# Weights of expert tiles taken by pairs from two shelves, in an attention and mixture-of-experts kernel

## What is computed

```python
x = x + attention(layernorm(x), ctx, ctx, w_proj, b_proj)     # x: 8 x 512 x 256, 16 heads of 16
z = layernorm(x)
gate_logits = z @ Wg.T                                        # 8 experts
gating = softmax over the two largest of them, 0 elsewhere
h = silu(z @ W1[e].T) * (z @ W2[e].T)                         # 682 hidden columns, per expert e
x = x + sum over e of gating[e] * (h @ W3[e].T)
```

## Time and profile before

| | us |
|---|---|
| median of three runs | 885.32 (885.25 to 887.26) |
| the profiled execution, its own time | 882.82 |
| its span, first to last instruction | 881.0 |

### The profile page before, as it was taken

The page is one execution under the profiler, slowest core; times in us unless marked ns, Lnnn a source line. Parts: engine busy times, 40 slices in busy tenths (PEclk is TensorE's granted clock), DMA queues, the critical chain, the costliest instruction groups (busy, mean ns, idle before and its releaser), DMA issues.

```text
span 881.0 us, 20060 instructions
## 1 busy us (share of the span) xinstructions
PE 786.4 (89%) x6472; PEld 481.1 (55%) x6472; DVE 602.0 (68%) x1224; ACT 557.1 (63%) x970; POOL 439.7 (50%) x431
## 2 busy tenths in 40 slices
PE   0578898989989898987989999997999999999995
PEld 0112233333333333322337788886888888888884
DVE  3888888989889898899725566553555555555553
ACT  3369789898898989867783544443444444444442
POOL 4565435787767778774634674223322222222222
PEclk9999999999999999999999999998999999999998
DMA  8585756867567685674184899999986688383832
GB/s 177 173 197 167 201 129 226 182 222 161 178 235 166 216 216 197 133 187 160 70 289 145 223 270 272 260 301 234 273 253 157 165 244 254 55 249 55 245 43 25
DMA packets 105955, 167.52 MB, mean 190 GB/s; under 512 B 54688, under 2 KB 83232, under 8 KB 101280
## 3 DMA queue, kind: packets, MB, share of 16 engines
q1 hardware_dynamic: 92448, 148.76, 58.9%
q0 software_dynamic: 13440, 17.90, 10.6%
HBM read 119.75 MB, written 42.55 MB: 184 GB/s over the span
## 4 chain that ended last, share of the span: by engine, by line
PE 39%; SPq 4%; issue 3%; ACT 3%; DMA 3%; POOL 2%; DVE 1%; POOLq 0%; ACTq 0%; DVEq 0%
PE ps L1371 8%; PE ps L1373 8%; PE ps L1375 8%; PE ps L1389 3%; PE ps L1393 3%; PE ps L1391 3%; PE ps L1294 2%; SPq L534 1%; ACT probs L839 1%; DMA slots<-fill 1%; DMA out<-y,aim 1%; POOL slots L472 1%; PE ps L1279 1%; PE ps L1398 1%; DMA w<-w_parts 1%
## 5 line engine op out<-in xcount | busy, mean ns | idle before, releaser
L970 DVE TENSOR_REDUCE neg_max<-ps 128x2 f16<-128x1024 f32 x256 | 309.2, 1221 | 35.5 <-PE ps L1266 31.0
L839 ACT ACTIVATE probs<-ps 128x1024 f32<-128x1024 f32 x256 | 259.0, 1024 | 59.4 <-PE ps L1279 58.9
L766 POOL DMA_INDIRECT out<-y,aim x72 | 113.4, 1575 | 247.6 <-DVE y L1197 174.9
L1371 PE MATMUL ps<-zt,w 128*128 128x256 f16 x792 | 216.9, 274 | 7.7 <-DMA w<-w_parts 5.8
L1373 PE MATMUL ps<-zt,w 128*128 128x256 f16 x792 | 216.7, 274 | 0.0
L1375 PE MATMUL ps<-zt,w 128*128 128x256 f16 x792 | 216.6, 274 | 0.0
L873 ACT ACTIVATE silu<-ps 128x256 f32<-128x256 f32 x216 | 82.6, 383 | 190.8 <-PE ps L1375 183.9
L1178 DVE SCALAR_TENSOR_TENSOR hid<-ps,silu 128x256 f32<-128x256 f32 x216 | 91.7, 425 | 134.4 <-ACT silu L873 130.2
L1294 PE MATMUL ps<-probs,v_ext 128*32 128x512 f32 x1024 | 138.1, 611 | 5.4 <-ACT heads L907 4.4
L1266 PE MATMUL ps<-k_stack,q_stack 48*128 48x512 f16 x512 | 104.1, 406 | 34.1 <-ACT probs L839 17.7
L1279 PE MATMUL ps<-q_stack,k_stack 49*128 49x512 f16 x512 | 101.7, 395 | 7.2 <-DVE neg_max L970 7.1
(11 more groups left out here) (126 smaller groups left out, 907.1 us busy)
## 6 DMA issues: line engine op xcount, KB each, us to landing
w<-w_parts SPq DMA_DIRECT2D x36, 1408.0 KB
w<-w_parts SPq DMA_DIRECT2D x36, 768.0 KB
w_in<-in_w SPq DMA_DIRECT2D x16, 704.0 KB, 5.2
v_ext<-in_v SPq DMA_DIRECT2D x8, 1024.0 KB, 5.4
k_stack<-k SPq DMA_DIRECT2D x48, 128.0 KB, 5.0
q_stack<-qt SPq DMA_DIRECT2D x48, 128.0 KB, 4.7
w_in<-in_w SPq DMA_DIRECT2D x8, 768.0 KB, 5.0
w_parts<-w_hi SPq DMA_DIRECT2D x16, 352.0 KB, 2.3
```

The source lines that it names most:

```text
L766: nc.gpsimd.indirect_dma_start(out=out, out_offset=bass.IndirectOffsetOnAxis(ap=aim[frm][:, t, 0:1].bitcast(U32), axis=0), in_=y[frm][:, t ...
L839: nc.scalar.activation(probs[g % 2][:, j:j + 2, k, :], pair_banks[PLACE["exp", u] % 3], ACT.Exp, scale=0.25).then_inc(s_exp, 1)
L970: nc.vector.tensor_reduce(neg_max[b % 2][:, i, c:c + 3:2], pair_banks[PLACE["max", u] % 3], AX.X, ALU.max, negate=True).then_inc(s_red, 1)
L1371: nc.tensor.matmul(dst, w[:, kk, 1, cols], z16[:, kk, :], start=(kk == 0), stop=False)
```

## The change

The two buffers of weights become shelves that hold a pair of tiles: tiles 2i and 2i+1 below 12 both use shelf i mod 2 (`shelf`). `new_tab` is 1 for an odd tile only if its expert isn't that of the tile before, and for an even tile from 4 on only if it isn't that of the tile three before, the last on this shelf. Tiles 0 and 2 and tile 12 load always; from tile 13 on all is as it was. The first tiles 0 and 2 are loaded ahead of the early pieces. Each shelf's loads are counted on four semaphores by k mod 4 (`landed`), since several tiles' loads may now be under way.

The order of SyncE's queue changes too: behind the up half of an even tile k it issues the up load of k+1 and the rows of k+2; behind that of an odd tile the rows of k+2 and the up load of k+3; behind the down half of an even tile the down load of k+1, of an odd one that of k+3. An odd tile's load waits until the tile before is done with the shelf, an even one's until tile k-3 is. The pads stand behind the steps of tiles 6 to 9. The first table has one instruction more.

```diff
+AT_PADS = EARLY
...
+def shelf(k, par, least):
+
+    return k // 2 % 2 if least < KNOWN else par
+
+
+def landed(f, k, half, par, least):
+
+    if least < KNOWN:
+        return f[k % 4], k // 4 * 16 + 16
+    return f[4 + par], half * 16 + (16 - 8 * KNOWN)
...
-        f_w = [sem("f_w0"), sem("f_w1")]
-        f_w3 = [sem("f_w3_0"), sem("f_w3_1")]
+        f_w = [sem(f"f_w{i}") for i in range(6)]
+        f_w3 = [sem(f"f_w3_{i}") for i in range(6)]
...
-        K_EARLY_TAB, K_TAB, K_BIAS = 18, 38, 9
+        K_EARLY_TAB, K_TAB, K_BIAS = 19, 39, 9
...
             def load_up(k, half, par, least):
                 e = sp.value_load(exp_tab[0:1, at(k)], min_val=0, max_val=E - 1)
                 new = sp.value_load(new_tab[0:1, at(k)], min_val=0, max_val=1)
-                if least >= 2:
+                if least >= KNOWN:
                     sp.wait_ge(f_up, (k - 1) * HC)
+                else:
+                    ge(sp, f_up, (k if k % 2 else k - 2) * HC)
                 hold(sp, s_held[3])
-                sp.dma_start(w12[par][:, :, :, :].rearrange("p k a h -> p (k a h)"),
+                sp.dma_start(w12[shelf(k, par, least)][:, :, :, :].rearrange("p k a h -> p (k a h)"),
                              w12_dram[bass.ds(e, 1)].rearrange("o p k a h -> p (o k a h)"), cond=new
-                             ).then_inc(f_w[par], 16)
+                             ).then_inc(landed(f_w, k, half, par, least)[0], 16)
...
             def load_down(k, half, par, least):
...
-                if least >= 2:
+                if least >= KNOWN:
                     sp.wait_ge(f_down, (k - 1) * SUB)
+                else:
+                    ge(sp, f_down, (k if k % 2 else k - 2) * SUB)
...
+            def known(load, k):
+                if k < KNOWN:
+                    load(k, k // 2, k % 2, k)
+
+            def behind_up(k):
+
+                if k % 2 == 0:
+                    known(load_up, k + 1)
+                known(load_rows, k + 2)
+                if k % 2:
+                    known(load_up, k + 3)
+
+            def behind_down(k):
+
+                known(load_down, k + 3 if k % 2 else k + 1)
+
             def load_ahead(k, half, par, least):
                 for _ in range(HC + 1):
                     yield
-                if least + 2 < EARLY:
-                    load_rows(k + 2, half + 1, par, least + 2)
-                    load_up(k + 2, half + 1, par, least + 2)
+                if k + 2 < EARLY:
+                    behind_up(k)
                 for _ in range(PIECES - HC - 1):
                     yield
-                if least + 2 < EARLY:
-                    load_down(k + 2, half + 1, par, least + 2)
+                if k + 2 < EARLY:
+                    behind_down(k)
...
                     if b == B - 1:
-                        load_up(1, 0, 1, 1)
-                        load_down(1, 0, 1, 1)
+                        load_up(2, 1, 0, 2)
+                        load_down(2, 1, 0, 2)
...
-            known_tiles(EARLY, EARLY + 2, load_rows, load_up, load_down)
-            sp.wait_ge(s_tab, K_EARLY_TAB + 1)
-            known_tiles(EARLY + 2, KNOWN, load_rows, load_up, load_down, pad_regions)
+            for k in range(EARLY - 2, KNOWN - 1):
+                behind_up(k)
+                behind_down(k)
+                if k == AT_PADS:
+                    sp.wait_ge(s_tab, K_EARLY_TAB + 1)
+                if AT_PADS <= k < AT_PADS + E // 2:
+                    pad_regions(2 * (k - AT_PADS), 2 * (k - AT_PADS) + 2)
             total = tiles_in_use(sp)
             sp.wait_ge(f_pad, 16 * E)
...
-                    step(nc.vector.memset(new_tab[:, 0:2], 1))
-                    yield
-                    step(tt(new_tab[:, 2:KNOWN], expert[:, 2:KNOWN], expert[:, 0:KNOWN - 2], ALU.not_equal))
+                    step(nc.vector.memset(new_tab[:, 0:KNOWN + 1], 1))
+                    yield
+                    step(tt(new_tab[:, 1:KNOWN:2], expert[:, 1:KNOWN:2], expert[:, 0:KNOWN:2], ALU.not_equal))
+                    yield
+                    step(tt(new_tab[:, 4:KNOWN:2], expert[:, 4:KNOWN:2], expert[:, 1:KNOWN - 3:2], ALU.not_equal))
...
-                pe.wait_ge(f_w[par], half * 16 + 16)
-                z16, w = zt16[par], w12[par]
+                pe.wait_ge(*landed(f_w, k, half, par, least))
+                z16, w, v = zt16[par], w12[shelf(k, par, least)], w3[shelf(k, par, least)]
...
-                pe.wait_ge(f_w3[par], half * 16 + 16)
+                pe.wait_ge(*landed(f_w3, k, half, par, least))
```

More of the change, by code:

```diff
@@ L550, in load_down @@
                 new = sp.value_load(new_tab[0:1, at(k)], min_val=0, max_val=1)
-                if least >= 2:
+                if least >= KNOWN:
                     sp.wait_ge(f_down, (k - 1) * SUB)
+                else:
+                    ge(sp, f_down, (k if k % 2 else k - 2) * SUB)
                 hold(sp, s_held[3])
-                sp.dma_start(w3[par][:, :, :, :].rearrange("p a m c -> p (a m c)"),
+                sp.dma_start(w3[shelf(k, par, least)][:, :, :, :].rearrange("p a m c -> p (a m c)"),
                              w3_dram[bass.ds(e, 1)].rearrange("o p a h -> p (o a h)"), cond=new
-                             ).then_inc(f_w3[par], 16)
+                             ).then_inc(landed(f_w3, k, half, par, least)[0], 16)
             def load_first_tiles():
@@ L645, in _, with pad_regions @@
                     if b == B - 1:
-                        load_up(1, 0, 1, 1)
-                        load_down(1, 0, 1, 1)
+                        load_up(2, 1, 0, 2)
+                        load_down(2, 1, 0, 2)
             for _ in early:
                 pass
[L651 to L654, removed]
+            def pad_regions(first, end):
+                for e in range(first, end):
+                    row = sp.value_load(pad_tab[0:1, e:e + 1], min_val=0, max_val=E * REGION)
+                    sp.dma_start(z_dram[bass.ds(row, SLOTS), :].rearrange("(s p) c -> p s c", p=P),
                                  fill[:, :, :]).then_inc(f_pad, 16)
-            known_tiles(EARLY, EARLY + 2, load_rows, load_up, load_down)
-            sp.wait_ge(s_tab, K_EARLY_TAB + 1)
-            known_tiles(EARLY + 2, KNOWN, load_rows, load_up, load_down, pad_regions)
+            for k in range(EARLY - 2, KNOWN - 1):
[5 more added lines that the diff above has]
+                    pad_regions(2 * (k - AT_PADS), 2 * (k - AT_PADS) + 2)
             total = tiles_in_use(sp)
@@ L1154, in table @@
                     yield
-                    step(tt(new_tab[:, some], expert[:, some], expert[:, KNOWN - 2:FFN_TILES - 2], ALU.not_equal))
+                    step(tt(new_tab[:, KNOWN + 1:FFN_TILES], expert[:, KNOWN + 1:FFN_TILES],
+                            expert[:, KNOWN - 1:FFN_TILES - 2], ALU.not_equal))
                     assert n_tab == K_TAB, n_tab
@@ L1388, in tile @@
                             h = [hid16[:, m, a, slots] for a in range(2)]
-                            nc.tensor.matmul(y_bank[t], h[1], w3[par][:, 0, m, :], start=first, stop=False,
+                            nc.tensor.matmul(y_bank[t], h[1], v[:, 0, m, :], start=first, stop=False,
                                              skip_group_check=True)
-                            nc.tensor.matmul(y_bank[t], h[0], w3[par][:, 1, m, :], start=False, stop=False,
+                            nc.tensor.matmul(y_bank[t], h[0], v[:, 1, m, :], start=False, stop=False,
                                              skip_group_check=True)
-                            nc.tensor.matmul(y_bank[t], h[0], w3[par][:, 0, m, :], start=False, stop=False,
+                            nc.tensor.matmul(y_bank[t], h[0], v[:, 0, m, :], start=False, stop=False,
                                              skip_group_check=True)
@@ L1397, in tile @@
                                 pe.wait_ge(f_tail, (k + 1) * 2)
-                            nc.tensor.matmul(y_bank[t], tail16[:, slots], w3[par][:, 1, m, :],
+                            nc.tensor.matmul(y_bank[t], tail16[:, slots], v[:, 1, m, :],
                                              start=False, stop=True, skip_group_check=True).then_inc(f_down, 1)
```

## The result

| | before | after |
|---|---|---|
| median, us (18 runs each) | 885.29 (881.98 to 889.34) | 879.12 (876.68 to 884.07) |
| profiled execution, us | 882.82 | 877.01 |
| its span, us | 881.0 | 875.2 |

The ratio of the times is 0.9934, with an interval of 0.9918 to 0.9949: 5.8 us less (4.5 to 7.3); the medians differ by 6.2. The forecast was 5.9 us less, 879.4.

What follows compares the result with a forecast made beforehand. Tile 12's late start, behind pads and a weight load, then a slow clock bounded the kernel. Terms -4.3 - 1.74 + 0.1 = -5.9 us gave 876.9 profiled, 879.4 as median (chance 0.60); range 877.0 to 882.5.

Steps and rivals of the forecast that it cites:

- What is skipped: Weight loads of tiles 0 to 11: six of twelve vanish, 13.4 MB; by itself this gives nothing, as TensorE waits for none.
- The pads: Pad transfers ahead of tile 12: issued sooner, out by about 582 us and, even at 8.3 us, down by 590.5.
- What is late next: SyncE's queue before tile 12: waits for tile 10's end, then 12.6 us; tile 12 starts at 604.1 instead of 608.40.
- The gap term: TensorE's idle time before tile 12: 4.3 us gained, a gap of 1.7 us left.
- The estimate of 5.3 us: Flight of tile 12's 1.44 MB weight load by the skill's fit; would gain 0.8 us more, but the sum used 6.11.
- The clock: TensorE behind the gap at tile 12: clock stays at full speed after a short gap, so 1.74 us come back.
- rival (a): At tile 12 the clock falls though the gap is short, so 1.7 us stay lost: 881.1 us, chance 0.14.
- The adds: Accumulating adds before tile 12: they speed up with fewer loads; tile 10's lands at 599 to 603 us, needed by 608.0.
- (c): Adds stay slow and VectorE's wait at tile 12 replaces the weights' wait: 884.7 us, chance 0.10.
- Odd tiles: Odd tiles' loads among the first twelve: passed over under the down half of the tile before, with 3.3 us to spare.
- (d): Word that an odd tile's weights are there comes late; a real load costs 2.9 us plus 1.7 of clock: 893, chance 0.06.
- The 0.1 us taken for the instruction more on the table: VectorE's first table: one more instruction, 0 to 0.3 us with its wait, taken as 0.1 us lost.

Runs made afterwards that it cites:

- the bytes alone: Kernel before in its own load order, with the weight loads of tiles 3, 5, 7, 9 and 11 passed over: 878.46 us, ratio 0.9928.

## Why the prediction was right, point by point

**What is skipped.** Six loads, 13.4 MB: right by the page's totals and by the short issues. The sentence that this alone gives nothing, since TensorE waits for none of these loads, was wrong: the experiment with the bytes alone gives the whole gain in the old order. The later points of the prediction did count what the bytes do to the pads and the adds, so the sum didn't suffer from it.

**The pads.** Forecast to be down by 590.5, they were down by 584.09. They landed in 2.7 to 7.8 us, median 3.3, instead of 8.1 to 10.1. The direction was right, the bound too careful, and it didn't matter: tile 10 ends later, at 589.96.

**What is late next.** SyncE's new wait for the end of tile 10, as forecast, in the order forecast:

| from tile 10's end, us | forecast | chain of after |
|---|---|---|
| to the transposes (592.31) | 2.2 | 2.35 |
| to the weight load (596.69) | 4.1 | 4.38 |
| to the matmul (602.77) | 6.25 | 6.08 |
| sum | 12.6 | 12.81 |

The flight stayed near 6 us, as taken: the down load and the add beside it were still there. Yet the gap, counted from step to step as the prediction counts it, is 2.27 us (2.11 of them idle) and not 1.7. Some 0.2 are the sum. The rest is tile 11: it lost its own late start of 0.20 us and began 0.36 us sooner relative to tile 10, so that it also ended sooner and waited longer. The gap term was 3.7 us (6.00 less 2.27) in place of 4.3.

The Trainium skill ("DMA: Bandwidth & Descriptors", section "Where 436 GB/s comes from") says that in a transfer between HBM and SBUF the side of the HBM, about 358 GB/s, sets the pace. With the fixed 2.0 us of the fit that the prediction cites (the same page of the Trainium skill, section "Anatomy of one DMA — SWDGE (gpsimd) path") that is an estimate of 6.0 us for 1.44 MB. The trace of after has 5.93 for tile 12's load, so there it agrees; but the up loads of tiles 0 to 10 in the same trace took 6.2 to 11.1 us, and tile 12's took 7.97 with the bytes alone, so the estimate doesn't tell what a load takes beside others. The estimate of 5.3 us in the prediction, from 436 GB/s, was met by no up load whose landing these traces show.

**The clock.** The term of 1.74 us came back in three executions of after out of four; in the first, 1.67 of it was lost, which is rival (a). The chances of 0.60 to 0.14 don't contradict that. The length of the gap doesn't tell them apart: 2.11 us where it fell, 2.10, 2.12 and 2.27 where it didn't. What decides stays open.

**The adds.** Tile 10's add was forecast for 599 to 603 and landed at 598.2; VectorE took up tile 12 at 601.56 without a wait. The landings' median of 4.5 us is near to the 3.7 without loads. That this step was needed, and that (c) is real, is shown by the sooner pads without fewer bytes: there the wait takes over. Its price in (c), 0.7 us less than before, is the outer end of what was measured there (from 0.7 us less to 3.4 more): VectorE's wait holds TensorE in the middle of a tile, and the clock falls there too, from 613.6 to 620.5 us, as it fell in the gap before.

**Odd tiles.** None waited. As a price, (d) was undersized: 2.9 us and 1.7 of clock a tile rest on the flight of 6.11 us; with real loads the flights took up to 9.5 us and the gaps of five tiles were 2.6 to 6.4.

**What wasn't counted.** Tile 11's 0.36 us, as above; and tile 4, in which VectorE's wait for GpSimd's sum of the softmax fell. GpSimd works it out behind two issues of adds that wait for the one before them to land; this one, issued at 508.18 us before and at 507.01 after, landed in 4.13 us instead of 5.00. Waits of VectorE in tile 4, before and after (total us, times, longest):

```profile
DVE z_row L1022 <- POOL den L723: 3.2, 1, 3.2
```

```profile
DVE z_row L1058 <- POOL den L759: 2.3, 1, 2.3
```

Tile 4 ran 516.07 to 527.32 before and 514.91 to 525.77 after, 0.39 us shorter. So 0.75 us were gained that I hadn't counted, against 0.6 less at the gap: that the sum of 5.9 us came out so well is luck, since two small misses cancel. The 0.1 us taken for the instruction more on the table can't be read from these executions: tile 0 starts up to 6 us apart in them. The profiled execution's own difference of 5.8 us is partly luck too: its clock term was missing, and its tile 0 started 1.14 us sooner (457.38 against 458.52), which no part of the change explains.

## What to carry to other kernels

Bytes that nothing waits for can still be worth their time: look at which short transfers share the queue with them, and whether a chain of dependent transfers (here the adds) is close to the pace of the engine that it feeds. If such a chain is behind, moving a wait sooner or later only moves the loss; count its period against the work per tile before any reordering. When an in-order queue gets a new wait, put what is urgent and already allowed in front of it: here that was worth another 2.3 us.

## What the runs showed of the hardware that I had not expected

The spread of the runs comes mostly from the attention stage. In the four executions of after the span from the start of tile 0 on is 416.3 to 417.8 us, but that start lies up to 6 us apart. In the second of them the clock was down in the attention stage four times, three times for 3.4 us and once for 6.8, in the windows around 246, 352, 400 and 413 us (three of them here):

```profile
246.00:256.00 10.00, 9.55 (x63) 2.76 (x61) 7.52 (x11) 8.28 (x12) 5.81 (x4) 0.83 0.39 154
350.00:358.00 8.00, 7.33 (x48) 2.25 (x46) 4.72 (x4) 6.29 (x9) 5.57 (x3) 0.79 0.43 151
...
413.00:417.00 4.00, 3.82 (x20) 0.95 (x20) 2.54 (x5) 1.82 (x3) 0.00 (x0) 0.57 0.00 0
```

In the first, as in that of before, it was down there once, at 407 to 411. The start of tile 0 lies at 457.38 us in the first and at 463.47 in the second, a spread as large as the whole gain. The two executions of before, at 458.52 and 459.76, lie inside it; two and four are too few to say that the change has no part in it.

The same 1408 KB load took 5.93 us at tile 12 in the kernel after, but 6.2 to 11.1 from issue to landing at the tiles ahead of it; 7.97 at tile 12 with the bytes alone; and 5.7 to 9.5 with real loads at every tile. And a load that is passed over costs 0.11 us or less of SyncE's time:

```profile
586.82 0.11 SPq L559 DMA_DIRECT2D w<-w_parts  x1
590.31 0.10 SPq L571 DMA_DIRECT2D w<-w_parts  x1
```
